# A SyncE queue in another order: weight loads ahead of the expert kits

## What is computed

```python
xn = layernorm(x)                                    # x: 2 x 1024 x 128
q, k, v = xn @ Wq.T + bq, xn @ Wk.T + bk, xn @ Wv.T + bv
attn = softmax(where(causal, q @ k.T * 128 ** -0.5, -inf)) @ v
probs = softmax(xn @ Wr + br)                        # 16 experts
topv, topi = top_k(probs, 2)
gate = sum(one_hot(topi, 16) * topv[..., None])
h = relu(xn @ W1[e] + b1[e])                         # 128 -> 512, each e
y = h @ W2[e] + b2[e]                                # 512 -> 128
out = x + attn + sum_e(gate[e] * y[e])
```

## Time and profile before

| | |
|---|---|
| time of the runs, median of 3 | 242.03 us (241.85 to 243.75) |
| span of the profiled execution | 237.6 us |
| own time of the profiled execution | not listed apart; the median less the span is 4.4 us |
| TensorE, VectorE, ScalarE, GpSimd busy | 73%, 57%, 50%, 51% of the span |
| granted TensorE clock, mean over the span | 0.898 |
| DMA, mean | 176 GB/s |

### The profile page before, as it was taken

One profiled execution on the slowest core, in us unless ns is written; L12 is line 12 of the kernel. 1 busy time (PEld: TensorE's weight loads), 2 busy tenths in 40 slices (PEclk: granted clock), 3 DMA queues, 4 the chain that ended last, 5 costly groups with the idle time before them and its releaser, 6 DMA issues.

```text
span 237.6 us, 5504 instructions
## 1 busy us (share of the span) xinstructions
PE 174.0 (73%) x1852; PEld 147.5 (62%) x1852; DVE 135.2 (57%) x318; ACT 119.0 (50%) x262; POOL 121.4 (51%) x146
## 2 busy tenths in 40 slices
PE   7549969759675002995989788988989879968940
PEld 7449645438474001874888777877878769855740
DVE  3893789798531004579768945444444543445491
ACT  1425496767541004496859546455464564544500
POOL 8593906388777770015049864534535445346250
PEclk9995597997958755599999999999999999999996
DMA  5879999419966110524995364653655554300682
GB/s 156 238 259 257 165 141 149 126 37 335 289 212 262 45 56 11 177 80 168 316 360 217 145 244 146 228 187 150 234 183 198 207 212 159 139 25 0 191 274 66
DMA packets 30202, 41.82 MB, mean 176 GB/s; under 512 B 5665, under 2 KB 18347, under 8 KB 29920
## 3 DMA queue, kind: packets, MB, share of 16 engines
q1 hardware_dynamic: 27648, 37.24, 52.6%
q0 software_dynamic: 2528, 4.24, 5.4%
HBM read 16.09 MB, written 9.39 MB: 107 GB/s over the span
## 4 chain that ended last, share of the span: by engine, by line
PE 37%; DVE 26%; another core or an unknown queue 17%; issue 10%; ACT 7%; DMA 1%; DVEq 0%; ACTq 0%
PE pO L1051 4%; DVE wts L755 4%; PE pS L1083 4%; DVE xn L651 4%; PE pS L1074 4%; PE pO L1005 4%; PE pS L974 3%; PE pS L1080 3%; PE pS L1081 3%; ACT xT L596 3%; PE pO L1053 2%; PE pO L1052 2%; PE pT L1039 2%; PE pT L987 2%
## 5 line engine op out<-in xcount | busy, mean ns | idle before, releaser
L478 POOL DMA_INDIRECT pairs_dram<-space,slot_space x47 | 48.8, 1038 | 56.4 <-ACT space L602 47.8
L855 DVE SCALAR_TENSOR_TENSOR xT<-pS,xT 128x512 f16<-128x512 f32 x47 | 32.5, 691 | 45.3 <-issue 22.9
L1051 PE MATMUL pO<-space,xT 128*128 128x128 f16 x188 | 38.5, 219 | 10.6 <-issue 6.0
L613 ACT ACTIVATE xT<-pS 128x512 f16<-128x512 f32 x47 | 27.9, 594 | 32.0 <-PE pS L1083 26.4
L467 POOL DMA_INDIRECT slots_dram<-slot_space,slotrow x32 | 34.6, 1080 | 14.8 <-issue 9.5
L1080 PE MATMUL pS<-xT,wts 128*128 128x128 f16 x188 | 38.8, 219 | 0.3 <-issue 0.3
L1083 PE MATMUL pS<-xT,wts 128*128 128x128 f16 x188 | 38.8, 219 | 0.0
L1081 PE MATMUL pS<-xT,wts 128*128 128x128 f16 x188 | 38.8, 219 | 0.0
L1052 PE MATMUL pO<-space,xT 128*128 128x128 f16 x188 | 38.5, 218 | 0.0
L1053 PE MATMUL pO<-space,xT 128*128 128x128 f16 x188 | 38.5, 218 | 0.0
L1051 PEld LDWEIGHTS pO<-space,xT 128*128 128x128 f16 x188 | 18.2, 97 | 15.0 <-issue 9.6
(11 more groups left out here) (144 smaller groups left out, 396.1 us busy)
## 6 DMA issues: line engine op xcount, KB each, us to landing
space<-wts SPq DMA_DIRECT2D x47, 352.5 KB
raw<-in_L_ffn_W SPq DMA_DIRECT2D x14, 512.0 KB, 5.3
slots_dram<-space SPq DMA_DIRECT2D x1, 3055.0 KB, 27.4
raw<-pairs_dram SPq DMA_DIRECT2D x8, 256.0 KB, 5.0
slot_space<-slots_dram SPq DMA_DIRECT2D x1, 1040.0 KB, 8.8
xin<-in_L_attn_x SPq DMA_DIRECT2D x4, 256.0 KB, 3.5
wts<-in_L_ffn_b SPq DMA_DIRECT2D x1, 1024.0 KB, 29.7
raw<-in_L_ffn_W SPq DMA_DIRECT2D x4, 256.0 KB, 2.9
```

The lines of the kernel that those rows point to most:

```text
L478: pool.indirect_dma_start(pairs_dram, bass.IndirectOffsetOnAxis(ap=slots_i[:, j, D:D + 1], axis=0), ybuf[:, j % NYB, :], None, bounds_chec ...
L613: nc.scalar.activation(hid[:, j % NHB, 0, :], pA(j), ACT.Relu).then_inc(hi_done, 1)
L855: dve.scalar_tensor_tensor(out=hid[:, j % NHB, 1, :], in0=pA(j), scalar=0.0, in1=hid[:, j % NHB, 0, :], op0=ALU.max, op1=ALU.subtract).the ...
L1051: pe.matmul(y, h_hi, w_hi, start=(c == 0), stop=False)
```

## The change

The five loads of weights 3 to 7 now stand together, ahead of the three waits. Kits 0 to 5 follow behind the waits as one row, then the wait for the scatters and the first reload, kit 6, weights 8, and the rest as before.

```diff
-            load_weights(RAW // 2)
+            for n in range(RAW // 2, len(WL) - 2):
+                load_weights(n)
             sp.wait_ge(expert_done, 1)
             sp.wait_ge(b2_in, 16)
             sp.wait_ge(blank_sent, 16)
-            for n in range(RAW // 2, E // 2 - 1):
-                for j in range(2 * n - RAW, min(2 * n - RAW + 2, NST - 1)):
-                    load_kit(j)
-                if n + 1 < E // 2 - 1:
-                    load_weights(n + 1)
+            for j in range(NST - 1):
+                load_kit(j)
 
             sp.wait_ge(rows_sent, 16 * K * NT)
             for n, (a, z) in enumerate(zip(XG, XG[1:])):
                 sp.dma_start(slots_i[:, a:z, :], slots_v[:, a:z, :]).then_inc(slots_in[n], 16)
                 if n == 0:
-                    load_weights(len(WL) - 3)
                     load_kit(NST - 1)
                     load_weights(len(WL) - 2)
```

## The result

| | before | changed |
|---|---|---|
| median of 4 runs | 241.94 us (241.06 to 243.75) | 246.53 us (245.49 to 248.75) |
| ratio | | 1.023, 95% interval 1.0149 to 1.0311 |
| span of the profiled execution | 237.6 us | 246.9 us |
| time of a run less its span | | 1.8 to 1.9 us |

The change costs **4.6 us**; the forecast was 6.4, the time 248.4. The spans differ by 9.3, twice as much. Only 1.8 to 1.9 us lie around a span, so the profiled execution of before was an early one (237.6 where the median implies 240.1) and that of the change a late one (246.9 where it implies 244.7). Steps are read from the profiles, the size of the whole from the medians. A run more than 1.5% above its kernel's fastest counts as slow: ratios and their intervals use the other runs alone, medians and ranges all of them.

A forecast was written before the change was run, and what follows sets the result against it. No engine was the bound: the chain of waits was spread over TensorE (37%) and VectorE (26%). Span 237.6 + 6.4 (late reload 4.9, clock 1.5) + 4.4 around the span = 248.4 us, range 236 to 253.

The forecast's parts named there:

- (a): SyncE's queue: loads of experts 8 to 13 moved ahead of the kits wait for the same low parts; worth nothing.
- (b): SyncE's queue: expert 14's load waits for the ninth low part, delaying six kits and first reload; +4.9 us (+4.4 to +9.3).
- (c): First expert tiles: TensorE, after idling, runs at the 1.2 GHz level; +1.5 us (0 to 3.4).
- shifts whole: Expert tile loop: a chain with no work that could run ahead, so all of it moves with its start.
- (d): DMA from 53 to 76 us: six kits' traffic leaves; nothing by itself, may touch the hold-up.
- the hold-up: Attention, 77.5 to 92.5 us: TensorE's signals come late, and TensorE, VectorE and ScalarE idle while GpSimd scatters rows.
- The base: Whole kernel: profiled span 237.6 us, with 4.4 us around it up to the median of 242.03.
- the forecast's case: Start of the expert stage: reload late, the hold-up stays; 245.5 to 253 us, chance 0.60.
- with the same length: Sign in the changed profile: the idle stretch of 77.5 to 92.5 us stays at its place, equally long.
- this faster side: Rival in attention: the hold-up shrinks, by at most 15.0 us, down to 233.4; over 1% faster, chance 0.20.

The follow-up runs named there:

- e2b: Changed kernel with the load of expert 14 alone put back behind the first reload: 235.58 us, 0.9885 of the kernel before.
- e3: Changed kernel with 24 matmuls that nobody reads ahead of the slot transposes: 210.36 us, 0.9992 of the kernel before.
- e1b: Changed kernel with the first reload ahead of the load of expert 14 and of all seven kits: 237.55 us (before 239.72).
- e4b: Kernel before with GpSimd's last 20 scatters in threes, each three behind one more finished attention tile: 229.55 us (before 239.72).
- e5: Kernel before with the first reload moved behind the load of expert 14, kits 0 to 5 early: 210.25 us, 1.0026 of before.

## Why the prediction was right, step by step

**(a) Earlier weight loads are worth nothing**: right. The two loads leave 0.03 us after their low parts (95.89 behind 95.86, 104.64 behind 104.61), as before.

**(b) The reload is held behind expert 14 and six kits, +4.9**: right as a mechanism, shown by e2b, and too small. From the ninth low part to the first tile it was 13.11 and 12.14 us in the two profiles, forecast 11.3, before 6.41: +6.7 and +5.7. Of the 1.8 us too few in the first, 1.0 is the second issue of expert 14 (1.46 us, taken as 0.43), 0.6 the kits with what lies between them (6.6 instead of 6.0), 0.4 the reload from issue to transposes (3.74 instead of 3.3), and copies and first tile gave 0.2 back. In the second profile that issue took 0.43, and 0.9 us were missing. The kits and the reload were inside the bounds given; the issue of expert 14 had been given none. By itself: the Trainium skill's formula (DMA: Bandwidth & Descriptors, the anatomy of one DMA) gave 2.9 us for this reload. Behind six kits it took 3.6 us to land in both profiles, and 3.74 and 3.70 to the transposes, so the 3.3 of the prediction's sum, worked out from the row of 256 KB, was nearer.

**(c) The clock, +1.5**: about right. From first tile to first relu it was 1.90 us against 1.13, and from there to tile 4's relu 9.37 in one profile and 124.87 - 116.46 = 8.41 in the other against 8.31: +1.8 and +0.9. That this is the clock's price is argued, not shown. The experiment meant for it, e3, ran where the start was not late; its matmuls were over 8.57 us before the transposes, and the granted clock was 0.50 from 88.2 to 98.4 in spite of them.

**The tile loop "shifts whole"**: nearly. From tile 4's relu to tile 46's it was 91.2 us before, 92.9 and 91.6 in the two profiles of the changed kernel. e2b, whose reload was not late, has 92.9 too, so the 1.7 us belong to the execution rather than to the queue.

**(d) Kit traffic gone from 53 to 76, nothing by itself, may touch the hold-up**: left open. It may be why the ninth low part ended 0.9 and 3.1 us earlier in the two changed profiles, and 5.6 in e2b, which shares the late kits. That would fit the medians, +4.6 and +4.5, which are below the +7.5 and +6.5 of the stretch to the first relu. It is argued from three profiles, not shown; before was profiled on another chip than the last two. That 248.4 came within 2 us of 246.53 is therefore in part luck: the late start cost more than forecast, and an earlier ninth low part, which the forecast did not have, took some of it back.

**The base.** 4.4 us around the span was wrong; it is 1.8 to 1.9, and the profiled execution was 2.5 us faster than the median. It did no harm, as the sum went on top of the median.

**The rivals.** The hold-up stayed in both profiles of the changed kernel, so the forecast's case decided. It was not "with the same length", though: TensorE idled 21.72 us in one and 16.18 in the other, against 16.14, and in the other it fell one low part further on. So a hold-up that shifts was no idle rival: e2b had it elsewhere, e1b in pieces, and e4b took out most of it. The prediction gave this faster side 0.20. It had no case for a chip on which the hold-up is absent and the change costs nothing.

## What to carry to other kernels

Before moving loads ahead in an in-order queue, compare each load's issue with the end of what frees its buffer: if they are 0.03 us apart, an earlier place gains nothing, and its wait then holds everything behind it. What the wait costs is the lateness of what stands behind it, less the slack that this had: here 15.25 us later for the reload, 6.6 of them felt. So read when the wait ends, when the one that it replaces ended, and when the data is first needed, and know in which executions that order turns round. The large idle stretch was worth more than the order of the queue: two lines that space the scatters gave 10 us where the reordered loads cost 4.6, though only where there is a hold-up (0.9991 without).

## What the runs showed of the chip

- The same kernel took 240 to 242 us in two of the comparisons and 210 in the two others, on other chips. ScalarE and VectorE waited up to 22.8 us for TensorE's signals in the first pair, and no such wait stands in the traces of the second. What in the chip makes it is not known from these runs.
- The hold-up is at most half of these 30 us. From tile 4's relu to tile 46's, the kernel before took 212.57 - 121.38 = 91.2 us; e5, the same kernel but for one load, took 182.62 - 106.55 = 76.1 on a 210 us chip, both at a granted clock of 1.00:

```profile
106.55 0.60 ACT L613 ACTIVATE xT<-pS 128x512 f16<-128x512 f32 x1 [1.51 <-PE pS L1083]
...
182.62 0.60 ACT L613 ACTIVATE xT<-pS 128x512 f16<-128x512 f32 x1 [0.68 <-PE pS L1083]
```

- The hold-up ends with the scatters, wherever it starts. In the profiles of before, of the changed kernel (two) and of e2b, the last scatter ended at 88.90, 88.00, 89.06 and 90.52, and the first row whose wait is named "remote" starts at 92.55, 91.86, 92.34 and 93.52, which is 3.0 to 3.9 us later (in e2b VectorE went on at 92.16 already, its wait named "issue"). That the scatters hold the signals fits this. It is not enough by itself: in e4b 17 scatters, and on the 210 us chips all of them, went as close together without such a wait. Fewer or smaller scatters were not tried.
- One issue of the same load took SyncE 0.43, 1.46 and 1.47 us in three profiles, with nothing in the rows to tell why.
